# Attention with 2048 context rows walked in halves of 1024, one head a slot, the fp16 probabilities copied from the fp32 exponentials on VectorE

## What is computed

```python
def _L0_xattn_ref(x, context, Wq, Wk, Wv, Wo, bo):    # x 8x128x512 (layer-normed), context 8x2048x384
    q = (x @ Wq).reshape(B, Nq, HEADS, DIM_HEAD)      # 8 heads of 64
    k = (context @ Wk).reshape(B, context.shape[1], HEADS, DIM_HEAD)
    v = (context @ Wv).reshape(B, context.shape[1], HEADS, DIM_HEAD)
    sim = jnp.einsum('bihd,bjhd->bhij', q, k) * SCALE
    attn = jax.nn.softmax(sim, axis=-1)
    out = jnp.einsum('bhij,bjhd->bihd', attn, v)
    return out.reshape(B, Nq, HEADS * DIM_HEAD) @ Wo + bo
```

## Time and profile before

| what | value |
|---|---|
| three runs | 918.46, 918.85, 920.45 us |
| median | 918.85 us |
| span of the profiled execution (first to last instruction) | 917.6 us |
| PE busy | 903.4 us, 98% of the span |
| ACT busy | 628.3 us, 68% |
| DVE busy | 590.5 us, 64% |
| POOL busy | 504.8 us, 55% |
| granted TensorE clock, mean | 1.000 |

### The profile page before, as it was taken

How to read it: one execution, slowest core, us unless ns; L and a number is a source line. 1 busy time by engine, 2 the same in 40 slices (tenths; PEclk the granted TensorE clock), 3 DMA queues, 4 the chain that set the end, 5 groups by cost and what they waited for, 6 DMA issues and landing times.

```text
span 917.6 us, 20100 instructions
## 1 busy us (share of the span) xinstructions
PE 903.4 (98%) x7470; PEld 564.5 (62%) x7470; DVE 590.5 (64%) x1069; ACT 628.3 (68%) x1398; POOL 504.8 (55%) x393
## 2 busy tenths in 40 slices
PE   6999999999999999999999999999999999999998
PEld 3556666666666666666666666666666455544444
DVE  6546666656666666666666666666667769886634
ACT  4857887777788788788878778877776523235540
POOL 4637656566556666666665655787777755310000
PEclk9999999999999999999999999999999999999999
DMA  9478677876767677677677868967999662333502
GB/s 333 98 142 167 135 129 141 163 145 139 136 142 131 135 146 138 132 137 141 134 143 152 157 130 140 194 133 146 186 190 165 105 133 64 72 86 74 183 13 80
DMA packets 340271, 126.38 MB, mean 138 GB/s; under 512 B 316113, under 2 KB 317905, under 8 KB 340177
## 3 DMA queue, kind: packets, MB, share of 16 engines
q1 hardware_dynamic: 325232, 96.66, 57.0%
q10 hardware_dynamic: 14944, 28.45, 9.6%
HBM read 45.36 MB, written 2.10 MB: 52 GB/s over the span
## 4 chain that ended last, share of the span: by engine, by line
PE 90%; DVE 3%; ACT 2%; SPq 2%; DMA 1%; issue 1%; ACTq 0%; DVEq 0%
PE v_ps L658 28%; PE k_ps L658 26%; PE e_ps L727 9%; PE e_ps L658 8%; PE o_ps L749 6%; PE o_ps L752 3%; PE e_ps L1014 3%; PE o_ps L1007 1%; PE e_ps L1007 1%; PE o_ps L768 1%; DMA raw<-in_ctx_t 1%; PE o_ps L947 1%; PE v_ps L1007 1%; DVE q_max L1531 1%; SPq L624 1%
## 5 line engine op out<-in xcount | busy, mean ns | idle before, releaser
L1984 POOL TENSOR_TENSOR p_l<-p_f,p_h 128x1024 f16<-128x1024 f32 x128 | 272.4, 2128 | 237.3 <-ACT p_f L1195 237.3
L1190 ACT ACTIVATE p_h<-e_ps,bias 128x512 f16<-128x512 f32 x256 | 175.7, 686 | 2.6 <-issue 0.5
L1195 ACT ACTIVATE p_f<-e_ps,bias 128x512 f32<-128x512 f32 x256 | 176.4, 689 | 0.0
L1526 DVE TENSOR_TENSOR k_l<-k_ps,k_h 128x512 f16<-128x512 f32 x128 | 88.5, 691 | 132.3 <-ACT k_h L1160 132.3
L1518 DVE TENSOR_TENSOR v<-v_ps,v 128x512 f16<-128x512 f32 x127 | 87.5, 689 | 107.0 <-ACT v L1152 107.0
L1531 DVE TENSOR_REDUCE q_max<-e_ps 128x2 f32<-128x1024 f32 x128 | 150.8, 1219 | 8.0 <-PE e_ps L727 0.9
L658 PE MATMUL v_ps<-wv_h,ctx_h 128*128 128x256 f16 x756 | 124.4, 273 | 1.2 <-DVE v L1518 1.1
L658 PE MATMUL v_ps<-wv_l,ctx_h 128*128 128x256 f16 x756 | 123.7, 273 | 0.0
L658 PE MATMUL v_ps<-wv_h,ctx_l 128*128 128x256 f16 x756 | 123.7, 273 | 0.0
L749 PE MATMUL o_ps<-v,pt_h 128*128 128x128 f16 x1024 | 104.2, 220 | 0.5 <-issue 0.5
L658 PE MATMUL k_ps<-ctx_h,wk_h 128*128 128x512 f16 x384 | 103.8, 379 | 0.0
(11 more groups left out here) (311 smaller groups left out, 1399.0 us busy)
## 6 DMA issues: line engine op xcount, KB each, us to landing
raw<-in_ctx_t ACTq DMA_DIRECT2D x26, 768.0 KB, 5.3
w_raw<-in_w_t SPq DMA_DIRECT2D x32, 256.0 KB, 3.8
raw<-in_ctx_t SPq DMA_DIRECT2D x5, 768.0 KB, 7.0
pt_h<-p_h SPq DMA_TRANSPOSE x128, 3.7
pt_l<-p_l SPq DMA_TRANSPOSE x128, 3.3
out<-xr SPq DMA_DIRECT2D x7, 256.0 KB, 2.0
x_in<-in_x SPq DMA_DIRECT2D x6, 256.0 KB, 11.0
o_all<-in_x ACTq DMA_DIRECT2D x6, 256.0 KB, 3.5
```

The source lines that it names most:

```text
L1190: act.activation(p_h[:, s % H_RING, h, :], e_ps[s % 2][:, h, :], ACT.Exp, scale=EXP_SCALE, bias=bias[:, n % 2, h, q:q + 1]).then_inc(p_hi, 1)
L1195: act.activation(p_f[:, s % F_RING, h, :], e_ps[s % 2][:, h, :], ACT.Exp, scale=EXP_SCALE, bias=bias[:, n % 2, h, q:q + 1], accum_out=p_su ...
L1526: dve.tensor_tensor(k_l[:, n % 2, cols], k_ps[:, :], k_h[:, n % 2, cols], ALU.subtract).then_inc(k_split, 1)
L1984: pool.tensor_tensor(p_l[:, s % L_RING, :, :], p_f[:, s % F_RING, :, :], p_h[:, s % H_RING, :, :], ALU.subtract).then_inc(p_split, 1)
```

## The change

A slot is now a batch, a **half** of the context (1024 rows), a pair and one **head**, in the order batch, half, pair, head: all eight heads go over the first half of the context, then all eight over the second. Two slots of a pair are a unit u. Slots whose half is the second are `behind(s)`: s mod 16 is 8 to 15.

- `scores(u)` fills the banks of both heads of a unit in one piece, and raises `e_filled` once for the two.
- One maximum of 1024 columns to one value for a slot. For a slot behind, DVE then takes the smaller of this (negated) maximum and that of the same head in the first half: `new_max`, a one-column operation on two SBUF columns (L1529 of the changed kernel), which waits for the reduction; ACT's bias waits for it. DVE does this for both slots of a unit in turn.
- ACT makes one exponential of 1024 columns in fp32 for a slot (`exps_full`), with its sum, and none in fp16. `p_h` is made by DVE as a cast of `p_f` (`p_high`), ahead of `v_low` in the step.
- The first half's output is copied into `acc` (now held for all 4 pairs and both heads); the second half's is added with one fade factor. The row sums are joined by `add_sums`, one column, two SBUF tensors.
- Keys are kept in a ring of 4 units. v's wait for free tiles, loads and weight halves near the start are moved to the new order: `ctx_high(2)` one step later, `wv_low(1)` and `wk_low(2)`, `wk_low(3)` earlier.
- The tail has one `scores(UNITS-1)` ahead of `fold(0)` instead of `scores(126)`, `fold(0)`, `scores(127)`.

The diff, its core:

```diff
+UNITS = SLOTS // 2
+PER_BATCH = SLOTS // B
+PER_HALF = PER_BATCH // 2
+K_RING = 4
...
+        def slot_of(s):
+            return s // PER_BATCH, s % PER_BATCH // PER_HALF, s % PER_HALF // 2, s % 2
+        def behind(s):
+            return s % PER_BATCH >= PER_HALF
...
-        ctx_behind = {0: 2, 1: 3, 5: 4}
-        load_behind = {6: EARLY_CTX}
+        ctx_behind = {1: 2, 2: 3, 5: 4}
+        load_behind = {4: EARLY_CTX, 6: EARLY_CTX + 1}
...
+            def scores(u):
+                b, _, p, _ = slot_of(2 * u)
+                pe.wait_ge(k_split, 2 * u + 2)
+                if u:
+                    pe.wait_ge(p_full, 2 * u)
...
+                for i in range(2):
+                    cols = slice(i * QW, i * QW + QW)
+                    for left, right, first, last in ((q_h, k_h, True, False), (q_h, k_l, False, False), (q_l, k_h, False, True)):
+                        for h, rows in enumerate(head_rows):
+                            mm = pe.matmul(e_ps[h][:, i, :], left[rows, p, tokens], right[rows, u % K_RING, cols],
+                                           start=first, stop=last)
                 mm.then_inc(e_filled, 1)
...
             weighted_values(SLOTS - PV_LAG)
-            scores(SLOTS - 2)
+            scores(UNITS - 1)
             fold(0)
-            scores(SLOTS - 1)
             project_out(0)
...
-                act.activation(p_h[:, s % H_RING, h, :], e_ps[s % 2][:, h, :], ACT.Exp, scale=EXP_SCALE,
-                               bias=bias[:, n % 2, h, q:q + 1]).then_inc(p_hi, 1)
...
+                act.activation(p_f[:, s % F_RING, :, :], e_ps[s % 2][:, :, :], ACT.Exp, scale=EXP_SCALE,
+                               bias=bias[:, col:col + 1], accum_out=p_sum[:, col:col + 1]).then_inc(p_full, 1)
...
+            def slot_maximum(s):
+                col, old = s % PER_BATCH, s % PER_BATCH - PER_HALF
+                dve.wait_ge(e_filled, s // 2 + 1)
+                ins = dve.tensor_reduce(q_max[:, col:col + 1], e_ps[s % 2][:, :, :].rearrange("p i n -> p (i n)"), AX, ALU.max,
+                                        negate=True)
+                if behind(s):
+                    ins.then_inc(e_reduced, 1)
+                    dve.wait_ge(e_reduced, s // PER_BATCH * PER_HALF + s % PER_HALF + 1)
+                    ins = dve.tensor_tensor(new_max[:, col:col + 1], q_max[:, col:col + 1], q_max[:, old:old + 1], ALU.min)
+                ins.then_inc(e_maxed, 1)
...
+            def p_high(s):
+                dve.wait_ge(p_full, s + 1)
+                if s >= H_RING:
+                    dve.wait_ge(pt_h_landed[(s - H_RING) % T_RING], 16 * ((s - H_RING) // T_RING) + 16)
+                dve.tensor_copy(p_h[:, s % H_RING, :, :], p_f[:, s % F_RING, :, :]).then_inc(p_hi, 1)
```

More of the change, by code:

```diff
@@ L723, in scores @@
                     pe.wait_ge(xt_split, 4)
[L724 to L728, removed]
+                tokens = slice(b * T, b * T + T)
+                for i in range(2):
[4 more added lines that the diff above has]
+                                           start=first, stop=last)
                 mm.then_inc(e_filled, 1)
             def weighted_values(s):
-                n, q = stage_of(s)
-                b, p = pair_of(n)
+                b, half, p, h = slot_of(s)
                 g = p // 2
@@ L744, in weighted_values @@
                     pe.wait_ge(q_split, 8)
[L745 to L754, removed]
+                acc_bank, head = o_ps[s % 2], 2 * (p % 2) + h
+                for j in range(2 * JT):
+                    tile = 2 * JT * half + j
+                    pe.matmul(acc_bank[:, 0:VW], pt_h[:, s % T_RING, j, :], v[g][:, tile, head, :],
+                              start=(j == 0), stop=False, skip_group_check=True)
+                    mm = pe.matmul(acc_bank[:, 0:DH], pt_l[:, s % T_RING, j, :], v[g][:, tile, head, 0:DH],
+                                   start=False, stop=(j == 2 * JT - 1), skip_group_check=True)
                 mm.then_inc(pv_done, 1)
@@ L1209, in _ @@
             ctx_high(1)
-            ctx_high(2)
             for i in range(3):
@@ L1555, in accumulate @@
[L1555 to L1567 removed]
+                new, total = o_ps[s % 2][:, 0:VW], acc[:, p, h, :]
@@ new lines, in accumulate @@
+                if half:
+                    dve.wait_ge(fade_ready, PER_HALF * b + s % PER_HALF + 1)
+                    dve.wait_ge(acc_ready, s - PER_HALF + 1)
+                    ins = dve.scalar_tensor_tensor(total, total, fade[:, col:col + 1], new, ALU.mult, ALU.add)
+                else:
+                    if b:
+                        dve.wait_ge(o_ready, PAIRS * (b - 1) + p + 1)
+                    ins = dve.tensor_copy(total, new)
+                ins.then_inc(acc_ready, 1)
+            def p_high(s):
[3 more added lines that the diff above has]
+                dve.tensor_copy(p_h[:, s % H_RING, :, :], p_f[:, s % F_RING, :, :]).then_inc(p_hi, 1)
@@ L1635, in _ @@
                     wk_low(1)
+                    wv_low(1)
+                elif 1 < s < PAIRS:
+                    wk_low(s)
             def turned_low(what, r):
@@ L2064, in _ @@
                 done = s - PV_LAG - 1
-                if done >= 0 and done % QUARTERS == 3:
-                    o_norm(done // QUARTERS)
+                if done >= 0 and stage_end(done) is not None:
+                    o_norm(stage_end(done))
                 for r in ADD_BIAS.get(s, ()):
```

247 lines of the change are left out of this document (103 added, 144 removed).

## The result

The changed kernel takes **959.63 us** (median of 4 runs, 959.06 to 960.26), the kernel before 918.84 on the same chip: a ratio of 1.0443, 95% interval 1.0428 to 1.0458. The prediction was 951 us, range 922 to 980. The profiled execution has a span of 956.8 us, 39.2 more than before, where 32 were forecast. So 7.2 of the 8.6 us by which the median lies over the forecast are in the span; the rest is the distance from span to median, 2.8 us here, where the prediction took 1.25 from before.

A forecast was written before the change was run, and what follows sets the result against it. PE's products were taken as the bound, busy 903.4 of 917.6 us. 917.6 + 27.8 (walk) + 3.9 (start) + 1.1 (tail) - 0.85 (p_faded) = 949.6 us of span; with 1.25 to the median, 951 us, range 922 to 980.

The forecast's parts named there:

- The central step: Odd steps meeting ctx_low: held new_max stalls PE 1.6 us at step 11, 1.94 at 15; held add_sums 0.5 at 19.
- 1 (a one-column operation slips through): Rival: POOL does not hold one-column operations, the 27.8 us are gone, start and tail stay; 923 us, chance 0.14.
- 2 (the cast at one column a cycle): Rival: DVE's cast takes 1.22 us, stalls in every unit, some 57 us; 980 us, chance 0.14.
- the exponential: ACT's exponential of 1024 columns, taken as 1.11 us from ACT's copies, bounds 0.69 and 1.38.
- Rivals 3 and 4: 3: faster, waits for DVE and ACT go, 917 at best, chance 0.05; 4: nothing to be measured, 919, chance 0.05.
- the tail: scores(63) needs the exponential of slot 125 and k_low(127) behind a cast: +1.1 us (0 to 3).
- the start: Step 3: cast of slot 0 stands ahead of v_low(4), 4.4 us once; less waits that go, +3.9 us.
- now waits for the cast but comes no later: POOL's p_low, 414.1 against 414.75, with its slot's product 8 us away: nothing.
- A held cast "I leave at nothing": First half, with ctx_low: cast held 0.4 us more, a stall of 0.1, left at nothing.
- the other reading that the prediction gives: By the skill's rule the cast would run after ctx_low, from 413.73 to 414.42, stall under 0.1 us.
- p_faded: In the kernel before, two waits for v_low, at 608 and 630 us, came from p_faded and go: -0.85 us.
- the signs that the prediction named: Dozens of v_low waits, most 1.5 to 2 us, total near 28; new_max near 1.9 in 14 cases; PE busy 903 us.

The follow-up runs named there:

- Run 1: Changed kernel with new_max made by a reduction over the two maxima instead of an operation with two SBUF inputs; 936.79 us, ratio 1.0196.
- Run 10: Changed kernel, two-input new_max kept, with POOL's ctx_low and ACT's load behind it one step later; 939.30 us, ratio 1.0220.
- run 9: Kernel of run 8 with weight_low back ahead of k_low, right behind the cast; 920.20 us, ratio 1.0014.
- run 4: Changed kernel with both edits, the reduction for new_max and the cast behind v_low; 923.85 us, ratio 1.0054.
- run 7: Kernel of run 4 with add_sums by tensor_scalar, its columns read through pointers, and weight_low behind k_low; 927.51 us, ratio 1.0090.
- run 3: Changed kernel with DVE's cast of the probabilities behind v_low instead of ahead of it; 949.35 us, ratio 1.0333.
- run 8: Kernel of run 7 with v_high(4) ahead of ACT's first bias, v_low(4) between DVE's first two maxima, k_low(3) ahead of the first cast; 926.05 us.
- Run 11: Kernel before the change, with p_faded, its sum and the reciprocal behind v_low instead of ahead of it; 917.78 us, ratio 0.9989.
- run 2: Changed kernel with new_max by tensor_scalar, the old maximum read as a scalar through a pointer; 938.56 us, ratio 1.0213.
- run 5: Kernel of run 4 with p_h made by a second ACT exponential and no cast on DVE; 924.36 us, ratio 1.0056.

## Why the prediction was right, and where it was short

**The central step held.** "Everything is behind it, on DVE and through the bias on ACT": per unit 1.6, 1.94 and 0.5 us were predicted, 1.53, 1.90 and 0.43 measured, at the steps named and at no others in batches 0 to 6, apart from 1.1 us of crumbs. The sum for them was 27.8 and is 26.6. Run 1 takes the hold away and the 24 us at steps 11 and 15 shrink to 3. Run 10 leaves the two inputs and takes the neighbour away, with the same effect on these steps. By rivals: 1 (a one-column operation slips through) is refuted by 1995 ns for one column; 2 (the cast at one column a cycle) by 0.695 us against the 0.69 taken; the exponential of 1.113 us was predicted as 1.11. Rivals 3 and 4 needed a free `new_max`, and even so run 9 doesn't get below before.

The Trainium skill (SBUF — State Buffer, section Who interferes with whom) says that a VectorE instruction with at most one SBUF input, outside the two-port modes, does not contend with GpSimd. Run 1 agrees, 157 ns at most. The same page, section Summary: rules for kernel authors, says that where a VectorE instruction has two SBUF inputs and GpSimd's reads SBUF, the second to issue blocks until the first has finished; by that rule a `weight_low` that starts ahead of `p_low` is safe, and 0.68 against 2.38 us in runs 4 and 7 agree.

**What was short: 7.2 us of the span**, 39.2 against 32.0. The missing terms are the last batch 5.5, the crumbs 1.1, step 7 in the first batch 0.9, the tail 1.0 and the start 0.5; against them stand 1.2 us less at steps 11, 15 and 19, and some 0.3 more from waits of before that are gone; these come to 7.5, 0.3 over by rounding.

- *The last batch, 5.5 us, had no term.* The sum ended the walk's stalls with steps 11, 15 and 19 and counted the last batch as before. There `weight_low` is one more DVE operation with two SBUF inputs. In the kernel before it ran in 0.68 us ahead of `p_low`; the change starts `p_low` when the cast ends, and `v_low` stands between the cast and `weight_low`, which is held for 2.3 to 2.6 us in 13 of 16 cases. Seven waits for `k_low`, 3.9 us, and one of 0.27 for `v_low`, with 0.17 more for each, make up the 5.5. The timelines of DVE, POOL and PE in the changed kernel show it:

```profile
694.03 0.68 DVE L1552 CAST p_h<-p_f 128x1024 f16<-128x1024 f32 x1
694.63 0.68 DVE L1510 TENSOR_TENSOR v<-v_ps,v 128x512 f16<-128x512 f32 x1
695.23 2.59 DVE L1571 SCALAR_TENSOR_TENSOR wo_l<-raw,wo_h 128x512 f16<-128x512 f32 x1
697.74 0.68 DVE L1517 TENSOR_TENSOR k_l<-k_ps,k_h 128x512 f16<-128x512 f32 x1
```
```profile
695.14 2.13 POOL L1974 TENSOR_TENSOR p_l<-p_f,p_h 128x1024 f16<-128x1024 f32 x1 [1.44 <-issue]
697.23 0.90 POOL L1981 TENSOR_TENSOR o_sum<-acc 128x128 f32<-128x128 f32 x1
```
```profile
698.57 0.81 PE L670 MATMUL k_ps<-ctx_h,wk_h 128*128 128x512 f16 x3 [0.81 <-DVE k_l L1517]
```

The prediction looked at `p_low` ("now waits for the cast but comes no later") only for its product, not for whom it holds. Two pairs that differ in the order alone settle this: 5.46 us in the changed kernel against 0.26 in run 3, and 4.7 in run 8 against the 1.23 of run 9, which are another wait.

- *A held cast "I leave at nothing".* At step 7 of the first batch POOL has `p_low` and `ctx_low` one after the other. Timelines of DVE and POOL:

```profile
75.77 2.04 DVE L1552 CAST p_h<-p_f 128x1024 f16<-128x1024 f32 x1 [0.18 <-ACT p_f L1194]
```
```profile
74.16 3.10 POOL L1964 TENSOR_TENSOR ctx_l<-raw,ctx_h 128x1536 f16<-128x1536 f32 x1
```

It cost 1.15 us where before had 0.27. The 0.82 us for a held copy, by the earlier trace rows, were no bound: POOL's operation ended 0.54 us after that copy began. The cast here ends 0.55 us after `ctx_low`, as in the other reading that the prediction gives, by which it works when `ctx_low` is through. Leaving it at nothing was right only for the steps in which `ctx_low` ends early.
- *The start*, +3.9 predicted, +4.4 measured, partly by luck. PE waited 4.07 us for `v_low(4)` behind the cast. Then the clock was down, which no term had: in the stretches of 45 to 46 and 46 to 48 us the granted clock (after the times of PE, PEld, DVE, ACT and POOL) is 0.50 and 0.57: the lower of its two levels, 1.2 GHz, in the first and for most of the second.

```profile
41.00:45.00 4.00, 0.03 (x1) 0.00 (x0) 2.15 (x4) 3.29 (x7) 3.12 (x2) 0.91 0.44 98
45.00:46.00 1.00, 0.89 (x5) 0.67 (x6) 1.00 (x2) 0.00 (x0) 1.00 (x1) 0.50 0.42 45
46.00:48.00 2.00, 2.00 (x13) 1.43 (x12) 1.63 (x2) 0.00 (x0) 0.84 (x2) 0.57 0.71 224
48.00:50.00 2.00, 2.00 (x13) 1.08 (x11) 0.69 (x1) 0.60 (x1) 1.91 (x1) 1.00 1.20 313
```

The 18 value products of `value_tiles` took from 45.11 to 48.33 where before they took from 41.47 to 43.44 (the earlier trace rows has the first): 1.25 us more. Earlier first scores (0.6) gave about half of it back.
- *The tail*, +1.1 predicted, about +2 measured (39.2 less the 37.1 that the walk has lost by its last full unit): besides `k_low(127)` behind a cast (0.94), `fold_low` (the row `f_l`) is late by a `new_max` that POOL holds for 1.59 us, and PE waits 1.56 for it where before it waited 0.18. The prediction had the first and not the second.
- *p_faded*, -0.85: those waits are gone in the changed kernel. Their two units were 0.59 us longer each, so the term was 1.2. Run 11, which takes them and the 0.27 near 79 us away, is 1.1 us faster (0.2 to 1.8 by its interval).

Of the signs that the prediction named, `new_max` (47 of 64 at 0.16 to 0.21 us, 14 at 1.81 to 1.99), the cast, the exponential, the 4.07 us at the start and the total of the waits for `v_low` (29.1) came. Of these 25 waits only seven lie between 1.5 and 2 us (1.74); seven more are of 1.36. PE's busy time did not stay at 903 us: it is 909.3, by an estimate some 5 us from 0.17 at each of some 30 more stalls and 1.25 from the lower clock.

What stays open: which of run 9's late steps behind the last full unit costs the 0.7 us there, and why single transpositions of `p_l` take 5 to 6 us to land instead of 3.

## What to carry to other kernels

Where POOL works beside DVE, list every DVE operation that has two SBUF tensors, however small, or copies wide tiles within SBUF, and ask what POOL does at that moment, in all stages and not only in the one under study; then follow what is queued behind it on DVE and who waits for it on other engines. A hold is avoided by the form (a reduction, a column read through a pointer), by starting ahead of POOL's operation, or by an order in which nothing urgent stands behind. And what starts POOL's operation is part of the count: one place in DVE's order, 0.6 us, took `weight_low` from 0.68 to 2.38 us in run 7.

## What was new about the hardware

- A second column read through a scalar pointer was not held as a second tensor is: 213 to 215 ns in run 2, and with two pointers 257 to 275 ns in run 7, in 64 places each, where the two-tensor forms took up to 1995 and 1484 ns.
- A copy of 1024 fp32 columns to fp16 can be held longer than anything else seen here: 3.58 us for 0.69 of work.
- The hold goes the other way too: where a `weight_low` is at work when `p_low` starts, the latter takes 2.45 us instead of 2.13 (run 4, at 708.54).
- The granted clock of PE fell to 0.50 at the stall of 4.07 us (changed kernel, runs 1, 2 and 10) and at one of 2.85 us (run 5), and stayed at 1.00 through the 14 stalls of 1.36 and 1.74 us of the changed kernel and one of 1.53 us in run 4. What a fall costs differs: in run 2 it lasted longer than in run 1 and took 1.1 us more.
